# Attention output stored as full tiles of 128 partitions; DVE subtracts the row extremes and ACT takes the exponential out of PSUM and evacuates the spread operands

## The reference

```python
x = L0_attn_x                                  # [32, 512, 256] float32
xn = _layernorm(x, axis=-1)
# attention: 16 heads of 16, relative positions
q, k, val = heads(xn @ Wq + bq), heads(xn @ Wk + bk), heads(xn @ Wv + bv)
pos = heads(sinusoid @ Wp + bp)
content_score = einsum('bhsp,bhtp->bhst', q + u, k)
pos_score = _relative_shift(einsum('bhsp,htp->bhst', q + v, pos))
weights = softmax((content_score + pos_score) / sqrt(16), axis=-1)
att = einsum('bhst,bhtp->bhsp', weights, val) -> [32, 512, 256] @ Wo + bo
# experts: 8, each takes the 128 best of a batch's 512 tokens (top_k of softmax(xn @ gate_w))
ffn = scatter_add(g * (gelu(xn[m] @ w1) @ w2))           # rounded to bfloat16
return x + att + ffn
```

## Time and profile before

| | |
|---|---|
| median of 3 runs | 4703.37 us (4697.26 to 4705.75) |
| the profiled execution's own time | 4700.11 us |
| its span, first to last instruction | 4698.3 us |
| PE, DVE, ACT, POOL busy | 92%, 78%, 72%, 26% of the span |
| moved by DMA | 1391.25 MB, 296 GB/s over the span |
| mean granted clock of PE | 0.964 |

### The profile page before, as it was taken

How to read it: one execution, slowest core, us unless ns; L and a number is a source line. 1 busy time by engine, 2 the same in 40 slices (tenths; PEclk the granted TensorE clock), 3 DMA queues, 4 the chain that set the end, 5 groups by cost and what they waited for, 6 DMA issues and landing times. The chain is left out here.

```text
span 4698.3 us, 122852 instructions
## 1 busy us (share of the span) xinstructions
PE 4345.4 (92%) x48308; PEld 3356.0 (71%) x48308; DVE 3677.5 (78%) x7571; ACT 3393.9 (72%) x5153; POOL 1241.4 (26%) x905
## 2 busy tenths in 40 slices
PE   7899999999999999998999898889999999999997
PEld 3466666666666666666666666668888888888886
DVE  7699999989999899999998998855665666644455
ACT  3599999989999898999999999844444444444454
POOL 0111111111111111111111111125556656544443
PEclk9899999999999999999999999989999999999999
DMA  8899999999999999999999999972555555433259
GB/s 313 339 391 389 387 388 392 387 385 391 390 386 385 381 394 384 389 392 391 386 395 385 385 392 390 384 249 53 131 138 124 138 124 137 107 56 87 47 169 316
DMA packets 467846, 1391.25 MB, mean 296 GB/s; under 512 B 59216, under 2 KB 136656, under 8 KB 467024
## 3 DMA queue, kind: packets, MB, share of 16 engines
q1 hardware_dynamic: 418128, 1316.25, 74.2%
q0 software_dynamic: 49152, 67.14, 8.4%
HBM read 708.93 MB, written 674.23 MB: 294 GB/s over the span
## 5 line engine op out<-in xcount | busy, mean ns | idle before, releaser
L761 DVE CUSTOM_DVE_ANT_0 att_shifted<-att_quad,att_shifted 128x512 f32<-128x512 f32 x2048 | 1337.6, 684 | 112.4 <-DMA att_shifted<-xs_d 75.7
L614 ACT ACTIVATE att_shifted<-att_shifted,att_mn 128x512 f32<-128x512 f32 x2048 | 1375.7, 732 | 0.9 <-DVE att_mn L761 0.9
L609 ACT ACTIVATE ring<-att_quad 128x1024 f32<-128x1024 f32 x1024 | 1055.1, 1030 | 257.8 <-PE att_quad L988 244.1
L999 PE MATMUL att_quad<-att_kd,att_qd 64*128 64x512 f32 x2048 | 848.0, 459 | 179.6 <-DVE att_mn L761 173.8
L1434 ACT ACTIVATE ffn_hp<-ffn_up 128x512 fp32r<-128x512 f32 x512 | 305.9, 597 | 845.4 <-PE ffn_up L1615 845.1
L1520 DVE TENSOR_TENSOR ffn_hp<-ring,ffn_hp 128x512 fp32r<-128x512 f32 x512 | 460.3, 899 | 570.2 <-ACT ring L1436 570.0
L988 PE MATMUL att_quad<-att_pos,att_qd 64*128 64x512 f32 x2048 | 861.7, 448 | 15.0 <-ACT ring L609 13.6
L1024 PEld LDWEIGHTS att_tp<-ident,att_shifted 64*128 64x128 f32 x8192 | 645.6, 142 | 272.2 <-ACT att_shifted L614 117.7
L1615 PE MATMUL ffn_up<-ffn_xp,ffn_w1p 128*128 128x512 f32 x3072 | 796.3, 395 | 2.8 <-DVE ffn_xp L1463 2.8
L1024 PE MATMUL att_tp<-ident,att_shifted 64*128 64x64 f32 x8192 | 725.5, 229 | 64.4 <-DVE att_pt L770 23.0
L1025 PE MATMUL att_tp<-ident,att_shifted 64*128 64x64 f32 x8192 | 774.9, 232 | 2.3 <-issue 2.1
(11 more groups left out here) (132 smaller groups left out, 5931.9 us busy)
## 6 DMA issues: line engine op xcount, KB each, us to landing
xs_d<-ring SPq DMA_DIRECT2D x1024, 513.0 KB, 8.5
att_shifted<-xs_d SPq DMA_DIRECT2D x1024, 512.0 KB, 8.8
att_shifted<-in_L_attn_x_dram SPq DMA_DIRECT2D x32, 512.0 KB, 7.4
xn_d<-att_shifted SPq DMA_DIRECT2D x32, 512.0 KB, 6.7
xt_d<-att_shifted SPq DMA_DIRECT2D x32, 512.0 KB, 8.0
gathered<-xt_d SPq DMA_DIRECT2D x32, 512.0 KB, 9.7
att_d<-att_osb SPq DMA_DIRECT2D x512, 32.0 KB
ring<-in_L_ffn_w_dram SPq DMA_DIRECT2D x16, 1024.0 KB, 6.9
```

The costliest lines, as they stand in the source:

```text
L609: act.activation(xo[:, kk % NW, 2 * half:2 * half + 2, 1:S + 1], xp[:, :, :], ACT.Copy).then_inc(x_out, 1)
L614: act.activation(shifted[:, kk % NX, t], shifted[:, kk % NX, t], ACT.Exp, bias=mn[:, kk % NX, t:t + 1], scale=-1.0).then_inc(exp_done, 1)
L761: dve.tensor_tensor_reduce(out=shifted[:, kk % NX, t], in0=sp_[:, t % 2], in1=shifted[:, kk % NX, t], scale=-0.25, scalar=-NEG, op0=ALU.ad ...
L999: pe.matmul(sp_[:, t % 2, :], qd[rows, n // GH % ND, t * P:(t + 1) * P], kd[rows, kk // GH % 2, :], start=True, stop=True).then_inc(s_full, 1)
```

## The change

In the attention phase:

- ACT no longer takes the exponential in SBUF. DVE subtracts the least of each row from each tile in SBUF (`subtract_least`), and PE turns the plain differences. ACT then takes exp(-x) while it copies each half of the turned tile from tp to pt (`exponential`, two a head of 128x1024); DVE's two copies and ACT's one are gone.
- ACT, not DVE, copies kd and qd from mp.
- osb is stored whole, 128 partitions of 512 elements (with the unused rows between the tiles), in one transfer for a quad, in a new layout of att_d; sums_d is gone, since the sums are rows of att_d.

In the expert phase the sums are read from att_d (one transfer), their inverses are stored in four transfers, and a batch of the attention output is loaded in 16 transfers, one for each head.

```diff
-        def first_keys(n):
-            at = n % 2 * TT
+        def turned_keys(n, half):
+            at = 2 if half else n % 2 * TT
             return pt[:, at:at + 2].rearrange("p c (t r n) -> p (c t) r n", t=TT, r=2)
...
 def store_o(i, q):
-                    for t in range(TT):
-                        sp.dma_start(dst[q % NQ, :, :, t * P:(t + 1) * P], osb[32 * t:32 * t + HD, q % 2]).then_inc(o_stored[q % 2], 16)
-                    for t in range(TT):
-                        row = 32 * t + HD
-                        sp.dma_start(sums_d[at].rearrange("o (q h) t -> (o q) h t", q=NQ)[q % NQ:q % NQ + 1, :, t * P:(t + 1) * P],
-                                     osb[row:row + 1, q % 2]).then_inc(o_stored[q % 2], 16)
+                    u = i * QUADS + q
+                    wait_alone(sp, o_out, u + 1)
+                    sp.dma_start(att_d[u], osb[:, q % 2].rearrange("p h n -> p (h n)")).then_inc(o_stored[q % 2], 16)
...
 ACT:
-                def exponential(i, kk, t):
-                    act.wait_ge(added, (i * BH + kk) * TT + t + 1)
-                    act.activation(shifted[:, kk % NX, t], shifted[:, kk % NX, t], ACT.Exp, bias=mn[:, kk % NX, t:t + 1],
-                                   scale=-1.0).then_inc(exp_done, 1)
+                def exponential(i, kk, half):
+                    n = i * BH + kk
+                    act.wait_ge(t_full, n * TT + 2 * (half + 1))
+                    wait(act, o_full, n - 1 + half)
+                    act.activation(turned_keys(n, half), tp[:, :, :].rearrange("p r (k n) -> p k r n", k=2 * TT), ACT.Exp,
+                                   scale=-1.0).then_inc(t_out, 1)
+                def qd_evacuate(i, g):
+                    v = i * GROUPS + g
+                    act.wait_ge(qd_full, v + 1)
+                    wait(act, s_full, (v - ND + 1) * GH * TT)
+                    act.activation(qd[:, v % ND], mp[:, :], ACT.Identity, bias=ones).then_inc(qd_out, 1)
...
 DVE:
+                def subtract_least(i, kk, t):
+                    dve.wait_ge(added, (i * BH + kk) * TT + t + 1)
+                    dve.tensor_scalar(shifted[:, kk % NX, t], shifted[:, kk % NX, t], mn[:, kk % NX, t:t + 1], None,
+                                      ALU.subtract).then_inc(lowered, 1)
...
                         add(i, kk, 1)
                         add(i, kk, 2)
-                        if turning:
-                            t_evacuate(i, kk - LAG, 0)
-                        if even is not None:
-                            kd_evacuate(i, even)
-                        if odd is not None:
-                            qd_evacuate(i, odd)
+                        subtract_least(i, kk, 0)
+                        subtract_least(i, kk, 1)
                         add(i, kk, 3)
                         if not (last and kk == BH - 1):
                             add(i, kk + 1, 0)
-                        if turning:
-                            t_evacuate(i, kk - LAG, 1)
+                        subtract_least(i, kk, 2)
+                        subtract_least(i, kk, 3)
...
 PE, turn:
-                    pe.wait_ge(exp_done, (n + 1) * TT)
-                    if half == 0:
-                        wait(pe, t_out_dve, n * 2)
-                        wait(pe, t_out_act, n)
-                    else:
-                        pe.wait_ge(t_out_dve, n * 2 + 1)
+                    pe.wait_ge(lowered, (n + 1) * TT)
+                    wait(pe, t_out, n * 2 + half)
...
 ffn_phase, load_mid:
-                    sp.dma_start(att[:, s], att_d[bass.ds(b, 1)].rearrange("o (c p) t -> p (o c) t", p=P)).then_inc(m_in[s], 16)
+                    for h in range(H):
+                        rows = att_d[b * NQ + h // QH].rearrange("(t r) n -> r t n", t=TT)[0:HD, :, h % QH * P:(h % QH + 1) * P]
+                        at = h % (H // DC) * HD
+                        sp.dma_start(att[at:at + HD, s, h // (H // DC)].rearrange("p (t n) -> p t n", t=TT), rows).then_inc(m_in[s], 16)
```

More of the change, by code:

```diff
@@ L137, in shape_constants, with attention_phase @@
     return sinusoid, ident, marks, spread
-def attention_phase(nc, x, gate_w, w, w1, w2, consts, xn_d, xt_d, xs_d, att_d, sums_d, shared):
+def attention_phase(nc, x, gate_w, w, w1, w2, consts, xn_d, xt_d, xs_d, att_d, shared):
     sin_d, ident_d, marks_d, spread_d = consts
@@ L652, in body @@
                         keys = key_tile(kk - 1, last) if kk else None
-                        if not (first and kk == 0):
-                            exponential(i, kk - 1, 1)
-                            exponential(i, kk - 1, 2)
+                        turning = not (first and kk < LAG)
+                        even, odd = even_group(kk, last), odd_group(kk, last)
                         if queries is not None:
@@ L661, in body @@
                             x_evacuate(i, kk + LEAD, 0)
-                        if not (first and kk == 0):
-                            exponential(i, kk - 1, 3)
-                            exponential(i, kk, 0)
+                        if turning:
+                            exponential(i, kk - LAG, 0)
+                        if even is not None:
+                            kd_evacuate(i, even)
+                        if odd is not None:
+                            qd_evacuate(i, odd)
                         if positions:
                             x_evacuate(i, kk + LEAD, 1)
-                        if not (first and kk < LAG):
-                            t_evacuate(i, kk - LAG)
+                        if turning:
+                            exponential(i, kk - LAG, 1)
                         if kk % QH == 2 and not (first and kk < QH):
@@ L673, in _ @@
                     body(i)
-                for t in range(1, TT):
-                    exponential(ITERS, -1, t)
                 for k in range(LAG):
-                    t_evacuate(ITERS, k - LAG)
+                    for half in range(2):
+                        exponential(ITERS, k - LAG, half)
                 o_evacuate(ITERS - 1, QUADS - 1)
@@ L879, in _ @@
                     body(i)
-                for k in range(LAG):
-                    for t in range(2):
-                        t_evacuate(ITERS, k - LAG, t)
             @block.tensor
@@ L1162, with ffn_phase @@
 CONST_LOADS = 1 + DC + 2 + 4 + 5 + 1
-def ffn_phase(nc, x, Wo, bo, w1, w2, xn_d, shared, ffn_d, att_d, sums_d, inv_d, mid_d, out):
+def ffn_phase(nc, x, Wo, bo, w1, w2, xn_d, shared, ffn_d, att_d, inv_d, mid_d, out):
     MIX = 1
@@ L1265, in load_w @@
                     load_second(sp, w2, e, w2s).then_inc(w2_in, 16)
-                flat = "b (g h) t -> (b g) (h t)"
-                sp.dma_start(sums[:, :], sums_d.rearrange(flat, g=P // B)).then_inc(sums_in, 16)
+                sum_rows = att_d.rearrange("u (t r) n -> u t r n", t=TT)[:, :, HD]
+                sp.dma_start(sums.rearrange("p (t n) -> p t n", t=TT), sum_rows).then_inc(sums_in, 16)
                 sp.wait_ge(cleared, 1)
@@ L1273, in _ @@
                 sp.wait_ge(inverted, 1)
-                sp.dma_start(inv_d.rearrange(flat, g=P // B), sums[:, :]).then_inc(inv_stored, 16)
+                for t in range(TT):
+                    of_t = inv_d.rearrange("b (q h) s -> (b q) h s", h=QH)[:, :, t * P:(t + 1) * P]
+                    sp.dma_start(of_t, sums[:, t * QH * P:(t + 1) * QH * P].rearrange("p (h n) -> p h n", h=QH)).then_inc(inv_stored, 16)
                 sp.dma_start(wo[:, :, :], Wo.rearrange("(c p) n -> p c n", p=P)).then_inc(wo_in, 16)
@@ L1647, in build @@
         attention_phase(nc, x, gate_w, weights, w1, w2, (c["sinusoid"], c["ident"], c["marks"], c["spread"]), xn_d, xt_d, xs_d,
-                        att_d, sums_d, shared)
-        ffn_phase(nc, x, Wo, bo, w1, w2, xn_d, shared, ffn_d, att_d, sums_d, inv_d, mid_d, out)
+                        att_d, shared)
+        ffn_phase(nc, x, Wo, bo, w1, w2, xn_d, shared, ffn_d, att_d, inv_d, mid_d, out)
 _INS = ["L0_attn_x", "L0_attn_Wq", "L0_attn_bq", "L0_attn_Wk", "L0_attn_bk", "L0_attn_Wv", "L0_attn_bv", "L0_attn_Wp",
```

48 lines of the change are left out of this document (14 added, 34 removed).

## The result

The changed kernel takes 4714.98 us (median of 7 runs, 4712.74 to 4721.01), the one before 4703.37 (7 runs beside it, 4692.98 to 4705.75). The ratio is 1.0033, 95% interval [1.0024, 1.0043]: slower by a third of a per cent, where the prediction had 1.2% faster. The profiled execution took 4718.35 us, its span is 4716.6.

What follows compares the result with a forecast made beforehand. Two nearly equal limits, DMA transfers and the engines' chain, were taken to bound the attention stage, PE the expert stage. 4700.11 - 54 (stores) - 4 (stage end) + 3 (expert stage) = 4645, as median 4649 us; range 4600 to 4720.

Steps and rivals of the forecast that it cites:

- the most that freeing the transfers alone can give: Attention stage: DVE waits only 75.7 us in the whole run for the read of shifted, taken as the limit.
- I take two thirds, 0.72 us: Attention stage's stores: two thirds of the 1.08 us loss a store goes with SyncE's gap, 0.72 us gained.
- The bytes: Attention stage's stores: 136 KB become 256 KB, 0.123 MB more at 408 GB/s, +0.30 us a store.
- Rival C: Attention stage's stores: the change brings bytes only and is slower, +38 us less 4, 4737; chance 0.12.
- the step to zero: Attention stage: lighter DVE and ACT give little by themselves, put at 0.
- rival D: DVE in the attention stage: subtractions take 0.75 us, DVE needs 5.5 us a head, +60 us, 4760; chance 0.05.
- the loop of 5.1 us through PE and ACT: Attention head: PE takes 3.06 us, then ACT evacuates (1.03) and exponentiates (1.03) before the next turn.
- Rival B: Attention stage: the engines' chain keeps the pace, only 10 to 30 us come out, about 4680; chance 0.15.
- The end of the stage: End of the attention stage: one issue replaces the last eight and saves 3.6 us, put at -4 us.
- The expert stage: Expert stage: 16 att_d load issues a batch, 6.5 to 9 us later on SyncE, nearly hidden: +3 us, up to +10.
- The signs named beforehand: Attention stage: one att_d issue a quad, 370 GB/s or more at stores, mean about 400, DVE's wait below 40 us.
- rival A: Attention stage: transfers recover part or all of their loss, 4603 with none left, 4680 if a third goes; chance 0.60.

Runs made afterwards that it cites:

- store_only: The kernel before with only the new store, its layout and the loads that belong to it, old division of work: 4722.88 us, 1.0047.
- compact_store_only: The kernel before, division of work unchanged, with att_d stored without unused partitions, 136 KB in five issues of 2 KB rows: 4692.81 us, 0.9981.
- store_gap14: The kernel before with only the new store, plus fourteen one-row issues of 512 B behind each store: 4803.41 us, 1.0219 to the kernel before.
- compact_light: The changed kernel with att_d stored without unused partitions, without the four subtractions a head and with one of four value matmuls: 4633.70 us, 0.9859.

## Why the prediction was wrong

**What bounds the kernel: half right.** There are two stages, and two limits that lie near each other in the first: taking transfers away gives 5.34 to 5.39 us a head, taking DVE's subtractions away 5.49 (with PE's clock lower), and neither alone gives the 5.08 us of the earlier trace rows as a mean; that was a head without a projection. One error was the yardstick. The 408 GB/s of one stretch was taken for the rate that transfers have when left alone, and everything below it for a loss caused by stores. But the fastest of 40 such stretches has 408 too, before and after alike, and the median 392. With the dips at the stores shallower the mean stayed. The 75.7 us that DVE waits for the read were also taken for "the most that freeing the transfers alone can give"; taking a quarter of the transfers from the kernel before gave 123.

**The step that failed: "I take two thirds, 0.72 us".** It is the share of the 1.08 us loss a store that was to go with SyncE's gap. The gap went, from 4.9 to 1.5 us, and the dips grew shallower with it. Of the 0.72 us some 0.07 to 0.10 came back: that is what five issues for eight, a gap of 3.0 us and the same bytes gain. How much lies between five issues and one no run prices with the bytes held equal; by the holds, up to 4.3 us, it is nothing measurable.

What held the transfers instead can be read from SyncE's waits between 1000 and 1600 us. L46 is the helper `wait` and L411 the write; both lines here are waits that ended with ACT's evacuation of position scores (ring). Before, then `store_only`:
```profile
SPq L46 <- ACT ring L609: 90.9, 56, 2.3
SPq L411 <- ACT ring L609: 85.7, 72, 3.1
...
SPq L46 <- ACT ring L603: 180.3, 106, 2.7
SPq L411 <- ACT ring L603: 146.2, 98, 3.6
```
Together SyncE waited for ACT 177 us with the gap of 4.9 us and 327 with 1.7; `compact_store_only`, at 3.0, lies between them with 232. The time that the gap gave back became waiting for ACT: the next write had nothing to carry yet. This also bears on why a gap or a dip of a few microseconds was nearly free, though that was not tested by itself.

**The bytes: right in sign, somewhat too large.** Put at 0.30 us for 0.123 MB, +38 us in all. Two pairs of kernels measure 31 us, 0.24 us a store. So `store_only` should be 31 - 9 = 22 us slower, which is what it measures; the sum closes because the three kernels were measured against one another, so it is no independent test. With -4 to -7 for the division of work the changed kernel is at 15 to 18; its own ratio says 16.

**Rival C was what happened.** It had 4737 and a chance of 0.12. Its point of decision, more than 0.78 us of loss a store remaining, was passed: by the mean of 390.3 against 408 about 1.0 of 1.08 remained. Its reason also held: a full share at 332 GB/s was not a mark of narrow transfers, for with one store of 128 partitions windows of 366 and 310 GB/s have shares of 1.00 and 1.01. The rule named beside it, from the Trainium skill, "DMA: Bandwidth & Descriptors", section "Specifications", that rows of 512 B are enough for the full rate, agrees with the 0.07 to 0.10 us a store that eight issues with such rows cost over five with 2 KB rows; no run here separates row size from number of issues.

**ACT, DVE and PE: durations right, the step to zero right, its reason not.** The exponential was put at 1.03 us and takes 1.023; qd on ACT 0.70 and takes 0.688; the subtraction 0.50 and takes 0.543 over the run, so rival D is out. The estimate of 0.42 us worked out from the Trainium skill, "VectorE: DVE Perf Modes", section "The perf-mode tier table", was too low; the measurement decides. ACT's and DVE's busy time is 4.74 and 4.65 us a head (502.28 and 493.30 over 106 heads). ACT's came down by 0.38 us a head and not by 0.8: the prediction took 731 ns for each exponential that goes, but 430 of them hold ACT busy for only 288.6 us, 0.67 each. Lighter engines were put at nothing and gave 4 to 7 us. But the loop of 5.1 us through PE and ACT is not what keeps the mean pace: with room in the transfers it is 5.39 us, and 5.34 in the old division, whose loop is another one. PE also waits little for the exponential ahead of a turn, 6.7 us in 600 (6.0 for DVE's copy before) and 12.2 with half the reads:
```profile
PE att_tp L1006 <- ACT att_pt L606: 6.7, 31, 0.2
```
With half the reads PE is busy 4.96 us a head, and 5.00 in the old division; DVE and ACT have 4.71 and 4.75, and 5.14 and 5.11. PE's work is the one that the two share, which fits with their equal pace; that it sets it was not tested. Rival B, the chain that keeps the pace, explains nothing here, since nothing was there to be gained beyond it.

**The end of the stage.** The -4 us of the last issues can't be told apart from the rest; no run has them alone. The expert stage starts its first load 3096.00 us in, where it was 3078.05, and runs 1620.6 us to the end of the span against 1620.3: the whole difference of the profiled executions arises ahead of it.

**The expert stage: right.** Sixteen issues take 8.1 to 9.2 us in SP's timeline (forecast 6.5 to 9), POOL's wait for landing grew from 38.2 to 157.8 us, and PE is still busy in 1199.51 of 1200 us. +3 us was allowed for it and 0.3 is seen.

**The signs named beforehand.** One issue a quad: seen. Windows of 370 GB/s or more at stores: at 17 of 26 stores, where the window begins at the issue. Mean rate of 400: no, 390. DVE's wait below 40 us in the run: no, 211.9. PE waiting for ACT where it waited for DVE: seen, and small. Holes of over 0.7 us with one issue, which were to show the prediction wrong, stand at 8 of 26 stores (under 360 GB/s); at the store with a gather (408 - 310) / 408 x 6 = 1.4 us.

**A sum.** In rival A "4680 if a third goes" does not follow from the prediction's terms: 128 x (0.36 - 0.30) = 8 us of gain, with -4 and +3, is about 4695. Even at one third of the loss the change would have been a gain too small to tell.

**Still open.** Why the mean is 390 GB/s whatever the stores do, and 396 with light engines. And why the old gap of 4.9 us costs 9 to 12 us over one of 3.0 while `store_gap14` with 5.0 costs 81 over `store_only`: the old issues carry 136 KB in that time and the new ones 7 KB behind a 256 KB store, but that this is the reason was not tried. Where between 4.3 and 7.0 us a hold without transfers begins to cost was not measured.

## What to carry to other kernels

When transfers bound a stage, take the mean rate over hundreds of microseconds as the yardstick and count bytes first: 2.0 to 2.2 us a MB held here through three sizes of store, while a dip of 1 to 2.6 us at each store was nearly free. Before merging issues, look at what the issuing engine waits for just behind them (here ACT), and try a longer gap to see whether its length costs at all: here 2.6 us more cost nothing measurable and 5.3 us more cost 1.5 us a store. Don't pay for fewer issues with unused partitions without pricing the bytes. A faster engine in a stage that ends elsewhere becomes idle time, here 518 us ahead of one instruction.

## What the runs showed of the hardware

- The mean rate of the mixed stream of reads and writes stayed at 388 to 390 GB/s in eleven kernels, with stores from 136 to 512 KB and gaps behind them from 1.5 to 4.9 us.
- A share of 0.89 to 0.91 of the DMA engines went with 310 to 313 GB/s, and 1.01 with 390: the column falls by a tenth where the traffic falls by a fifth.
- SyncE's one-row issues take 0.30 us each (4.26 us for fourteen), its wide ones 0.32 to 1.34 us in the stretches shown after the change.
- A hundred empty instructions in a row on SyncE did not delay its next issue (1.7 us with and without them); the trace does not list them.
- In `compact_light`, where PE does fewer value matmuls, the granted clock fell to 0.87 in the window and 0.91 over the run, against 0.96 and 0.97, and a matmul of the content scores took 494 ns in place of 462.
